# GCN layers: ten feature blocks of a layer kept, sums by destination block, turns and products between the sums

## What is computed

```python
def gcn_conv(x, W, b, src, dst, n_nodes):
    h = x @ W
    deg = jax.ops.segment_sum(jnp.ones_like(dst, dtype=h.dtype), dst, num_segments=n_nodes)
    dinv = jnp.where(deg > 0, jax.lax.rsqrt(deg), 0.0)
    norm = dinv[src] * dinv[dst]
    msgs = h[src] * norm[:, None]
    out = jax.ops.segment_sum(msgs, dst, num_segments=n_nodes)
    return out + b
...
h = gcn_conv(x, W1, b1, src, dst, n)
h = jax.nn.relu(h)
out = gcn_conv(h, W2, b2, src, dst, n)
return out
...
x = _layernorm(x + _L1_gnn_ref(x, L1_gnn_W1, L1_gnn_b1, L1_gnn_W2, L1_gnn_b2, edge_index), axis=-1)
```

## Time and profile before

| | |
|---|---|
| three runs, median (lowest to highest) | 1476.71 us (1476.68 to 1478.66) |
| span of the profiled execution | 1478.3 us |
| PE busy | 1385.0 us (94%) |
| DVE busy | 771.6 us (52%) |
| POOL busy | 547.0 us (37%) |
| ACT busy | 445.6 us (30%) |

### The profile page before, as it was taken

How to read it: one execution, slowest core, us unless ns; L and a number is a source line. 1 busy time by engine, 2 the same in 40 slices (tenths; PEclk the granted TensorE clock), 3 DMA queues, 4 the chain that set the end, 5 groups by cost and what they waited for, 6 DMA issues and landing times.

```text
span 1478.3 us, 22402 instructions
## 1 busy us (share of the span) xinstructions
PE 1385.0 (94%) x7674; PEld 1283.9 (87%) x7674; DVE 771.6 (52%) x1843; ACT 445.6 (30%) x953; POOL 547.0 (37%) x626
## 2 busy tenths in 40 slices
PE   5999999999999999999999899889998999878797
PEld 3677999999999999999999899879888987777784
DVE  7876755234444365662223444645464615599544
ACT  2555421101100011100100311244574334557631
POOL 8001344242425243343434242034334454436630
PEclk9999999999999999999999999999999999967799
DMA  3111111122344142341212121122102211200001
GB/s 114 54 29 37 33 41 56 33 60 69 97 128 117 40 141 66 104 129 53 65 32 65 53 61 37 39 81 69 41 23 62 88 43 38 75 1 1 1 11 53
DMA packets 57782, 86.47 MB, mean 58 GB/s; under 512 B 6447, under 2 KB 54438, under 8 KB 57563
## 3 DMA queue, kind: packets, MB, share of 16 engines
q1 hardware_dynamic: 45184, 65.82, 15.2%
q10 hardware_dynamic: 12504, 19.36, 4.4%
HBM read 83.24 MB, written 1.92 MB: 58 GB/s over the span
## 4 chain that ended last, share of the span: by engine, by line
PE 76%; DVE 11%; ACT 4%; POOL 4%; issue 3%; DMA 2%; DVEq 0%; ACTq 0%; SPq 0%; POOLq 0%
PE psum L2448 13%; PE psum L2452 13%; PE psum L2451 13%; PE psum L2465 8%; PE psum L2468 8%; PE psum L2926 4%; PE psum L2588 2%; DVE max_scratch L2153 2%; PE psum L2513 2%; POOL w_lo L911 2%; PE psum L2827 1%; PE psum L2976 1%; PE psum L2831 1%; PE psum L2832 1%; PE psum L2437 1%
## 5 line engine op out<-in xcount | busy, mean ns | idle before, releaser
L2448 PE MATMUL psum<-w_lo,xT_hi 128*125 128x384 f32 (+5 forms) x1140 | 389.6, 342 | 7.2 <-DVE x_nat L1879 2.3
L2451 PE MATMUL psum<-w_hi,xT_lo 128*125 128x384 f32 (+5 forms) x1140 | 385.0, 338 | 0.0
L2452 PE MATMUL psum<-w_hi,xT_hi 128*125 128x384 f32 (+5 forms) x1140 | 384.9, 338 | 0.0
L898 POOL CAST w_hi<-w_raw 128x384 fp32r<-128x384 f32 x190 | 104.5, 550 | 590.2 <-PE psum L2452 482.6
L2448 PEld LDWEIGHTS psum<-w_lo,xT_hi 128*125 128x125 f32 (+1 forms) x1140 | 213.0, 187 | 10.7 <-POOL w_lo L911 3.4
L1083 ACT ACTIVATE h_hi<-psum 125x384 fp32r<-125x384 f32 (+1 forms) x120 | 59.1, 492 | 532.2 <-PE psum L2452 527.8
L1721 DVE TENSOR_TENSOR h_lo<-psum,h_hi 125x384 fp32r<-125x384 f32 (+1 forms) x120 | 66.9, 558 | 285.8 <-ACT h_hi L1083 284.5
L2451 PEld LDWEIGHTS psum<-w_hi,xT_lo 128*125 128x125 f32 (+1 forms) x1140 | 213.3, 187 | 0.4
L2452 PEld LDWEIGHTS psum<-w_hi,xT_hi 128*125 128x125 f32 (+1 forms) x1140 | 212.9, 187 | 0.0
L900 POOL TENSOR_TENSOR w_lo<-w_raw,w_hi 128x384 fp32r<-128x384 f32 x190 | 200.9, 1058 | 15.2
L2465 PE MATMUL psum<-h_lo,adjacency 125*125 125x384 f32 (+3 forms) x600 | 203.6, 339 | 2.3 <-issue 1.9
(11 more groups left out here) (348 smaller groups left out, 2220.9 us busy)
## 6 DMA issues: line engine op xcount, KB each, us to landing
w_raw<-weights_dram SPq DMA_DIRECT2D x296, 192.0 KB, 2.4
score_w_raw<-weights_dram ACTq DMA_DIRECT2D x58, 192.0 KB, 2.7
x_nat<-x_dram SPq DMA_DIRECT2D x1, 1875.0 KB
x_residual<-x_dram SPq DMA_DIRECT2D x1, 1875.0 KB
score_a_rows<-L_gnn_a_src_dram ACTq DMA_DIRECT2D x8, 192.0 KB, 3.6
score_a_rows<-L_gnn_a_dst_dram ACTq DMA_DIRECT2D x8, 192.0 KB, 5.0
out_dram<-x_residual SPq DMA_DIRECT2D x4, 375.0 KB
rgcn_bias<-rgcn_bias_dram SPq DMA_DIRECT2D x1, 1125.0 KB
```

Of the source, the lines that this page charges most:

```text
L898: nc.gpsimd.tensor_copy(mem.wh[:, slot, :], mem.raw[:, raw_slot, :]).then_inc(w_hi_ready, 1)
L2448: ins = nc.tensor.matmul(o, h, wl, start=(j == 0), stop=False, skip_group_check=True)
L2451: nc.tensor.matmul(o, l, wh, start=False, stop=False, skip_group_check=True)
L2452: ins = nc.tensor.matmul(o, h, wh, start=False, stop=stop and j == k - 1, skip_group_check=True)
```

## The change

All ten products of a layer keep their split parts (`gh`, `gl`, ten slots each, in place of two). The sums are then made by destination block: `gcn_sum(layer, f, m)` runs over the five source blocks for one bank, ten matmuls, and releases that bank. In each layer the five products of the first half come first; then each product of the second half is followed by one sum of the first half; then come the five sums of the second half. In layer 0 the ten groups of turns stand behind these last sums, first-half groups ahead (`G_UNITS`, `G_BEHIND`), the tenth behind the first product of layer 1; a product of layer 1 waits for the two groups of its own block. In layer 1 the turns for Q0 start ahead of the fifth sum. DVE and ACT follow the same order, ACT's wait ahead of two parameter loads asks for fewer sums, and `mask_diagonal` gets another address.

```diff
-        self.diag = at("mask_diagonal", [128, BP], F32, ah + 68928)
+        self.diag = at("mask_diagonal", [128, BP], F32, al + 31104)
+        self.gh = at("gcn_h_hi", [128, 2 * NB, HX], F32R, al)
+        self.gl = at("gcn_h_lo", [128, 2 * NB, HX], F32R, al + 15488)
...
+        G_UNITS = [(0, 0), (1, 0), (2, 0), (0, 1), (3, 0), (1, 1), (4, 0), (2, 1), (3, 1), (4, 1)]
+        G_BANKS = [5, 6, 7, 5, 6, 7, 0, 1, 2, 3]
+        G_BEHIND = {0: (0,), 1: (1,), 2: (2, 3), 3: (4, 5), 4: (6, 7, 8)}
...
+            def gcn_hi(layer, n):
+
+                act.wait_ge(h_done, H_L1 + layer * 2 * NB + n + 1)
+                s = n % NB
+                nc.scalar.activation(gcn_slot(mem.gh, s, n), bank(ring_bank(n), 0, HW, span(s)), ACT.Copy,
+                                     scale=mem.dinv[0:span(s), s:s + 1]).then_inc(h_hi_ready, 1)
+
+            def turn_hi_g(p):
+
+                act.wait_ge(turned, T_L1 + p + 1)
+                u = unit(KC, *G_UNITS[p])
+                nc.scalar.activation(unit_out(mem.xh, u), unit_in(G_BANKS[p], u), ACT.Relu).then_inc(xT_hi_ready, 1)
+
             for layer in range(2):
-                for i in range(2 * NB):
-                    h_hi(H_L1 + layer * 2 * NB + i, i % NB, i, mem.dinv)
+                for n in range(2 * NB):
+                    gcn_hi(layer, n)
                 if layer == 0:
-                    for m in range(NB):
-                        turn_hi(T_L1, KC, mem.xh, ACT.Relu, m)
+                    for p in range(UNITS):
+                        turn_hi_g(p)
...
-            act.wait_ge(out_done, OUT_L1 + 4 * NB)
+            act.wait_ge(out_done, OUT_L1 + NB)
             act.wait_ge(sums_moved, 1)
...
+            def gcn_h_lo(layer, n):
+
+                dve.wait_ge(h_hi_ready, H_L1 + layer * 2 * NB + n + 1)
+                s = n % NB
+                p = span(s)
+                nc.vector.scalar_tensor_tensor(gcn_slot(mem.gl, s, n), bank(ring_bank(n), 0, HW, p), mem.dinv[0:p, s:s + 1],
+                                               gcn_slot(mem.gh, s, n).bitcast(F32), ALU.mult, ALU.subtract
+                                               ).then_inc(h_lo_ready, 1)
+                for k in masks_at(layer, n):
+                    masks(k)
+
...
-                for f in range(2):
-                    for i in range(NB):
-                        h_lo(H_L1 + layer * 2 * NB + f * NB + i, i, f * NB + i, mem.dinv)
-                        for n in masks_at(layer, f * NB + i):
-                            masks(n)
-                        if layer == 1 and f == 1:
-                            dve.wait_ge(out_read, OUT_L1 + 3 * NB)
-                            res_first_half(i, mem.bias1[0:BP, 1, HW:D])
-                    if f == 0:
-                        for m in range(NB):
-                            gcn_sums(layer, f, m, mem.bias1[0:BP, layer, 0:HW])
-                    elif layer == 0:
-                        in_steps((lambda m: gcn_sums(0, 1, m, mem.bias1[0:BP, 0, HW:D]), 0),
-                                 (lo(T_L1, relu=True), 2))
-                        dve.wait_ge(xT_lo_ready, T_L1 + UNITS)
-                        extra_columns()
+                for n in range(NB):
+                    gcn_h_lo(layer, n)
+                for m in range(NB):
+                    gcn_h_lo(layer, NB + m)
+                    n = gcn_sums(layer, 0, m, mem.bias1[0:BP, layer, 0:HW])
+                    if layer:
+                        dve.wait_ge(out_read, n)
+                        res_first_half(m, mem.bias1[0:BP, 1, HW:D])
+                if layer == 0:
+                    for m in range(NB):
+                        gcn_sums(0, 1, m, mem.bias1[0:BP, 0, HW:D])
+                        for p in G_BEHIND[m]:
+                            turn_lo_g(p)
+                    turn_lo_g(UNITS - 1)
+                    dve.wait_ge(xT_lo_ready, T_L1 + UNITS)
+                    extra_columns()
...
-            def agg1(layer, f, s, after_gemm):
-                n = f * NB + s
-                i = H_L1 + layer * 2 * NB + n
-                if layer == 0 and n == 0:
-                    pe.wait_ge(xT_lo_ready, T_L1)
-                if layer == 0 and s == NB - 1:
-                    pe.wait_ge(over_read, 2 * NREL + 3)
-                aggregate(mem.ch, s, i % 2, i, after_gemm, OUT_L1 + (layer * 2 + f - 1) * NB)
+            def gcn_sum(layer, f, m):
+
+                if m == 0:
+                    pe.wait_ge(h_lo_ready, H_L1 + layer * 2 * NB + (f + 1) * NB)
+                    if layer == 0 and f == 0:
+                        pe.wait_ge(xT_lo_ready, T_L1)
+                        pe.wait_ge(over_read, 2 * NREL + 3)
+                pe.wait_ge(out_read, OUT_L1 + (layer * 2 + f - 1) * NB + m + 1)
+                o = bank(m, 0, HW)
+                for s in range(NB):
+                    a = mem.ch[0:span(s), s, nodes(m)]
+                    ins = nc.tensor.matmul(o, a, gcn_slot(mem.gl, s, f * NB + s), start=(s == 0), stop=False, skip_group_check=True)
+                    if f and m == 0 and s == 0:
+                        ins.then_inc(w_used, 1)
+                    ins = nc.tensor.matmul(o, a, gcn_slot(mem.gh, s, f * NB + s), start=False, stop=(s == NB - 1),
+                                           skip_group_check=True)
+                ins.then_inc(out_done, 1)
...
                 if n >= 2:
                     pe.wait_ge(h_lo_ready, H_L1 + layer * 2 * NB + n - 1)
-                elif layer:
-                    pe.wait_ge(xT_lo_ready, T_L1 + UNITS)
-                else:
+                elif layer == 0:
                     pe.wait_ge(root_read, (RLAYERS - 1) * 2 * NB - 1 + n)
                 if layer == 0 and f == 0:
                     pe.wait_ge(xT_lo_ready, T_L1 - UNITS + 2 * (s + 1))
+                elif f == 0:
+                    pe.wait_ge(xT_lo_ready, T_L1 + max(G_UNITS.index((s, 0)), G_UNITS.index((s, 1))) + 1)
                 if s == NB - 1:
                     pe.wait_ge(extra_ready, 4 * (RLAYERS + 1 + layer))
                 c = BASE_L1 + (layer * 2 + f) * KC
                 gemm_block(bank(ring_bank(n), 0, HW, span(s)), mem.xh, mem.xl, s, KC, c, c, HW, True,
-                           owed=(layer == 0 and n == 0), cols=nodes_x).then_inc(h_done, 1)
+                           owed=(n == NB or layer + n == 0), cols=nodes_x).then_inc(h_done, 1)
...
+            def gcn_turn(p):
+
+                m, i = G_UNITS[p]
+                pe.wait_ge(out_read, OUT_L1 + i * NB + m + 1)
+                used = [v for v in range(p) if G_BANKS[v] == G_BANKS[p]]
+                if used:
+                    pe.wait_ge(xT_lo_ready, T_L1 + used[-1] + 1)
+                if G_BANKS[p] == 7:
+                    pe.wait_ge(mask_read, sum(len(masks_at(0, n)) for n in range(2 * NB)))
+                b = G_BANKS[p] * 512
+                for j, (c, _) in enumerate(unit(KC, m, i)):
+                    ins = nc.tensor.transpose(ps[:, b + j * BP:b + (j + 1) * BP], of(mem.xn)(m, c), mem.ident[0:BP, 0:BP])
+                ins.then_inc(turned, 1)
+
+            def gcn_step(layer, f, s):
+
+                gcn_product(layer, f, s)
+                for n in masks_at(layer, f * NB + s):
+                    mask_row(n)
+
             for layer in range(2):
-                if layer:
+                for s in range(NB):
+                    if layer or s >= 2:
+                        gcn_step(layer, 0, s)
+                    if layer and s == 0:
+                        gcn_turn(UNITS - 1)
+                for m in range(NB):
+                    gcn_step(layer, 1, m)
+                    gcn_sum(layer, 0, m)
+                if layer == 0:
                     for m in range(NB):
-                        pe.wait_ge(out_read, OUT_L1 + NB + m + 1)
-                        turn(KC, of(mem.xn), T_L1, m)
-                for f in range(2):
-                    for s in range(NB):
-                        if layer or f or s >= 2:
-                            gcn_product(layer, f, s)
-                        for n in masks_at(layer, f * NB + s):
-                            mask_row(n)
-                        if s:
-                            agg1(layer, f, s - 1, s == NB - 1)
-                    agg1(layer, f, NB - 1, False)
+                        gcn_sum(0, 1, m)
+                        for p in G_BEHIND[m]:
+                            gcn_turn(p)
...
-            in_steps((turn_normed(1, T_Q[0]), 0), (q0_begin, 1))
+            turn_q0 = turn_normed(1, T_Q[0])
+            for m in range(NB):
+                if m == NB - 1:
+                    pe.wait_ge(mask_read, 2 * NB)
+                    turn_q0(0)
+                gcn_sum(1, 1, m)
+            for m in range(NB):
+                if m < NB - 1:
+                    turn_q0(m + 1)
+                q0_begin(m)
             chunks_and_scores(Q0, mem.xh, mem.xl)
 
```

8 lines of the change are left out of this document (added).

## The result

The changed kernel takes **1462.05 us** (median of four runs, 1461.34 to 1463.10) against 1476.70 for the kernel before (four runs, 1471.74 to 1478.66) on the same chip: a ratio of 0.9898, 95% interval [0.9882, 0.9914], or 14.65 us less. The forecast was 1465.5 with a range from 1462.5 to 1472.5. The interval of the ratio is 2.4 us wide to either side: the forecast itself (0.9924) lies outside it, the lower end of the range (0.9904) inside.

The account below looks back on a forecast made before the run. TensorE, busy 94% of 1478.3 us, was taken as the bound, with gains only at the two layers' ends: 3.9 + 5.2 + 2.1 = 11.2 us, from 1476.7 to 1465.5 us, range 1462.5 to 1472.5.

Parts of the forecast that it names:

- Seam A: End of layer 0 to layer 1's first product: turns among sums remove gaps, 7.18 us becomes 3.3, 3.9 us won.
- Seam B: End of layer 1 to the next layer's entry: 5.2 us of waits and 2.1 of clock, 7.3 us won.
- the faster block: First matmul block after layer 1: full clock takes it from 5.40 to 3.30 us, 2.1 us won.
- The thin place: End of layer 1: block 1's normalised rows ready at 9.5 us, TensorE there at 9.6; a few tenths may be lost.
- The inside: Within the layers, between their ends: moved work costs nothing to 2 us, taken as nothing; a gain is excluded.
- Q0: Next layer's entry, behind layer 1: its 4.6 us wait for split scores moves with TensorE and stays as long.
- (1): Rival, end of layer 1: cover only partial, a 2 us gap remains, clock falls; 3.2 us won there, 1469.6; chance 0.12.
- (2): Rival, behind layer 1: the 4.6 us score-split wait grows and takes back that end's gain; 1472.8 us; chance 0.08.
- (3): Rival, both layers' tails: clock drops among short groups, 100 matmuls lose 14 us, 1479.5 us; chance 0.04.
- The base of the forecast: Profiled execution of the kernel before, 1478.3 us, taken as 1.6 above the three-run median of 1476.7.
- The 3.0 us wait ahead of the first sum: Layer 0, waiting for the first h split: a product waits there instead of a sum, nothing won.
- low-clock stretches elsewhere, like the one behind 834, getting shorter: Case of a larger gain than any term gives, from half-rate stretches outside the two layer ends; chance 0.04.

Follow-up runs that it names:

- the filled kernel: Changed kernel plus fifteen unread matmuls in TensorE's 2.9 us wait ahead of layer 0's third product: 1463.25 us (1461.42 to 1463.61).
- the filled one: Kernel before plus fifteen unread matmuls in TensorE's 3.0 us wait ahead of the first GCN sum: 1473.82 us, ratio 0.9981.

## Why the prediction was wrong

**Seam A** (3.9, ends 2.8 to 4.4) was right. With a cold start on both sides a to b goes from 55.0 to 50.7, with a warm start on both from 52.28 to 47.95: 4.3 us each time. Three of the thirty turns now stand behind b and cost 0.3 us there, so the seam is worth 4.0. Undoing it cost 4.4 in the medians, 3.5 by the runs without the low clock among the turns.

**Seam B** (7.3, ends 3.5 to 7.6) was right: b to c goes from 64.5 to 57.46, 7.0 us in every trace, and 7.3 without the three turns of seam A in it; 2.1 of them are the faster block. Undoing it cost 5.7 in the trace and 4.3 in the medians, below the term but inside its ends. The thin place had the slack that was worked out, 0.1 us.

**The inside and Q0** were right: no wait inside, the waits of 0.9 and 4.4 us stay, c to d is 22.6 before and after (22.84 in the first trace before). Rivals (1), (2) and (3) did not come: 1.00 through all the short groups of both tails in the four traces of the changed kernel between 850 us and c.

The sum of the terms is then 11.3 us by the traces, 11.2 in the forecast, and 1465.5 is what the kernel gave on three of four occasions. That it came within 0.3 us is in part luck, for runs of one occasion differ by 2 to 6 us. The base of the forecast was read wrongly, without harm to the sum: the 1.6 us by which the profiled execution lay above the median set a span against times (it was about 3.5), and the term dropped out again.

**What failed** are two steps beside the sum. The 3.0 us wait ahead of the first sum was put down as "nothing won", and the low clock behind it, which the earlier trace rows shows and which the price of rival (3) was taken from, was carried over as a fixed part of both kernels. It is not: with the same wait and the same work the 73 instructions took 15.67 and 15.60 us in two traces of the changed kernel (mean clock 0.80 and 0.81), 14.46 in one (0.88) and 12.92 in the first (1.00). That is 2.75 us between the ends. The case was named ("low-clock stretches elsewhere, like the one behind 834, getting shorter") but with a chance of 0.04, as if the change had to shorten them; they differ from trace to trace without any change. The second is the lower end, 1462.5, put there because "the runs shown spread over 2 us". Three runs had shown 2 us; 17 of the same kernel on one occasion went from 1473.56 to 1483.15. The ends of the terms gave 1464.7; with 2.75 us for the start at a and the 3 us by which d to end differs between two traces of one kernel (501.4 and 498.3), the lower end belonged between 1459 and 1462.

What made the median of the first four runs low stays open in part. That all four were warm at a is not shown: one of them has a trace, which is warm, and all four lie where the filled kernel lies. Against it, that trace is the only warm one of the seven without a filler that have this wait (the three with a part put back took 15.53, 14.34 and 14.46 us for the same stretch), so four warm starts in a row would be rare unless runs of one occasion go together; and 2.75 us do not reach the whole 3.5. The mean clocks of the runs do not tell either: 0.976 and 0.977 in the four, 0.971 to 0.978 in the sixteen, where 1465.06 us goes with 0.972 and 1466.44 with 0.975. Nor is it settled what decides the clock at a. The Trainium skill, "TensorE: Matmul & The Clock Gate" (Part 1: The HAM clock gate, What's actually happening), says of a kernel's start that the chip's watch over activity runs free of the kernel, so that the same program is slow for a different number of matmuls from run to run. The traces show a spread of that kind at a wait in mid-kernel: 15.67, 15.60, 14.46 and 12.92 us for the same stretch. The Trainium skill's rule on transposes, on the same page (Part 4: PE-mode transpose), which the prediction set aside for the 1.00 in the earlier trace rows, would fit the trace with seam A put back (0.78) but none of the three traces of the kernel before, the filled one included (1.00). No run here tells the turns from the gaps between them, and with one trace of seam A put back it is not shown whether chance or that edit made the difference.

## What to carry to other kernels

Count a low-clock stretch behind a wait of some 3 us as a risk with a price, on both sides of the comparison, and not as a part of the kernel: look at more than one trace before it goes into the range or is left out of it. When sums over several accumulators end together, running them one accumulator at a time gives the engines behind them work while the rest is summed, and the first step of the next stage belongs between them where an engine's program order makes it a gate for the following block. A wait on TensorE that can't be removed can be filled with matmuls that nobody reads; on the kernel before, one such filler took 3.4 us off the median, on the changed kernel 2.1.

## What was not expected of the hardware

The granted clock behind one wait of 2.92 us, over the same 73 instructions, had a mean of 0.80, 0.81, 0.88 and 1.00 in four traces of one kernel. Fifteen matmuls of no use in that wait, 2.87 us, left a gap of 0.3 us, and the clock stayed at 1.00 in all four traces that had them. Over thirty turns with gaps of 0.4 to 1.2 us it was 1.00 in three traces of the kernel before and 0.78 on average in the one of the changed kernel with seam A put back.
